# Local-attention mask: one ScalarE copy per tile instead of two TensorE products

## The reference

```python
bk2, bv2 = (look(bk), look(bv))          # keys and values of the window before and of this one
mask = (it < jb) | (it > jb + w) | (jb == -1)
sim = jnp.einsum('bhwie,bhwje->bhwij', bq, bk2) * QK_SCALE
sim = jnp.where(mask, -jnp.finfo(sim.dtype).max, sim)
attn = jax.nn.softmax(sim, -1)
```

## Time and profile before

| | |
|---|---|
| Time, median of 3 runs | 1971.37 us (1968.38 to 1974.22) |
| Profiled execution: its time, its span | 1970.89 us, 1969.1 us |
| PE, PEld busy | 1816.7 us (92%), 1289.9 us (66%) |
| DVE busy | 1503.1 us (76%) |
| ACT busy | 1322.5 us (67%) |
| POOL busy | 1397.8 us (71%) |
| Mean granted clock of TensorE | 0.991 |

### The profile page before, as it was taken

How to read it: one execution, slowest core, us unless ns; L and a number is a source line. 1 busy time by engine, 2 the same in 40 slices (tenths; PEclk the granted TensorE clock), 3 DMA queues, 4 the chain that set the end, 5 groups by cost and what they waited for, 6 DMA issues and landing times.

```text
span 1969.1 us, 70556 instructions
## 1 busy us (share of the span) xinstructions
PE 1816.7 (92%) x29444; PEld 1289.9 (66%) x29444; DVE 1503.1 (76%) x2292; ACT 1322.5 (67%) x2146; POOL 1397.8 (71%) x1492
## 2 busy tenths in 40 slices
PE   7888788789999999999999999999999999999996
PEld 5666656456667666766676666666766667667664
DVE  5866867678887887787878877778787787877873
ACT  4666767466677667666766776677767766776663
POOL 3322323888888778888778877788877888877871
PEclk9999999999999999999999999999999999999998
DMA  5000000000001000010000000000100000000000
GB/s 174 2 0 0 0 1 2 1 5 9 3 3 47 3 2 14 3 48 2 3 14 2 24 26 3 14 2 3 47 3 2 14 2 3 3 2 2 8 2 18
DMA packets 12453, 25.44 MB, mean 13 GB/s; under 512 B 1856, under 2 KB 9728, under 8 KB 10496
## 3 DMA queue, kind: packets, MB, share of 16 engines
q1 hardware_dynamic: 12160, 21.18, 3.2%
HBM read 20.13 MB, written 1.05 MB: 11 GB/s over the span
## 4 chain that ended last, share of the span: by engine, by line
PE 64%; ACT 7%; issue 7%; DVE 3%; POOL 1%; DVEq 0%; POOLq 0%; ACTq 0%
PE banks L1140 22%; PE banks L1401 15%; PE banks L1342 10%; PE banks L1425 8%; PE banks L1387 6%; PE banks L1376 2%; ACT L813 1%; ACT arena L707 1%; DVE arena L1005 1%; ACT arena L813 1%; ACT L816 1%; DVE small L1034 1%; ACT arena L718 1%; PE banks L1447 1%; ACT arena L747 0%
## 5 line engine op out<-in xcount | busy, mean ns | idle before, releaser
L1401 PE MATMUL banks<-M,xs 128*32 128x512 f32 x3072 | 367.8, 595 | 0.3 <-DVE prob L1058 0.2
L475 POOL TENSOR_TENSOR arena<-arena 128x1024 f32<-128x1024 f32 x96 | 229.8, 2394 | 152.0 <-DVE arena L1005 152.0
L747 ACT ACTIVATE arena<-banks 128x1024 f32<-128x1024 f32 x192 | 197.3, 1028 | 118.4 <-PE banks L1401 117.1
L1052 DVE TENSOR_REDUCE small<-banks 128x16 f32<-128x1024 f32 x96 | 117.5, 1224 | 203.0 <-PE banks L1387 203.0
L1000 DVE TENSOR_TENSOR arena<-banks,tabs 128x1024 f32<-128x1024 f32 x192 | 233.3, 1215 | 39.7 <-ACT arena L707 31.4
L1005 DVE TENSOR_TENSOR arena<-banks,tabs 128x1024 f32<-128x1024 f32 x192 | 232.7, 1212 | 0.0
L480 POOL TENSOR_TENSOR arena<-arena 128x1024 f32<-128x1024 f32 x96 | 229.2, 2387 | 0.0
L1425 PE MATMUL banks<-arena 128*32 128x128 f32 x6144 | 189.4, 275 | 14.6 <-DVE arena L1091 14.1
L1342 PE MATMUL banks<-cst,arena 128*128 128x128 f32 x1536 | 201.4, 274 | 0.1
L470 POOL TENSOR_TENSOR prob<-prob,small 128x1024 f32<-128x1024 f32 x96 | 184.1, 1918 | 14.0 <-DVE small L1042 14.0
L1342 PEld LDWEIGHTS banks<-cst,arena 128*128 128x128 f32 x1536 | 177.8, 141 | 23.6 <-issue 2.9
(11 more groups left out here) (130 smaller groups left out, 4135.1 us busy)
## 6 DMA issues: line engine op xcount, KB each, us to landing
arena<-in_wvo_dram SPq DMA_DIRECT2D x6, 1024.0 KB, 5.1
qkraw<-in_wqk_dram SPq DMA_DIRECT2D x6, 1024.0 KB, 4.8
W<-in_w_dram SPq DMA_DIRECT2D x6, 341.0 KB, 3.2
W<-in_w_dram SPq DMA_DIRECT2D x6, 192.0 KB, 2.4
res<-in_x_dram SPq DMA_DIRECT2D x4, 256.0 KB, 3.6
tabc<-in_tab_dram SPq DMA_DIRECT2D x1, 1024.0 KB, 9.1
out_dram<-res SPq DMA_DIRECT2D x4, 256.0 KB, 2.9
sca_s<-in_sca_dram SPq DMA_DIRECT2D x6, 128.0 KB, 4.8
```

Of the source, the lines that this page charges most:

```text
L475: pool.tensor_tensor(kc, kc, ks, ALU.add).then_inc(s["k_add"], 1)
L747: act.activation(vw[:, (2 * k + g) % RV, :], two(V_BANK), ACT.Copy).then_inc(s[f"v_cp{g}"], 1)
L1401: ins = pe.matmul(bk(V_BANK + z)[WIN * q:WIN * (q + 1), :], xs[:, b, t0:t0 + WIN], M[:, q, :, :].rearrange("p m n -> p (m n)"), start=True ...
```

## The change

`mask_scores` moves from PE to ACT. The two products of PE per tile go; ACT writes the pattern, read from the float32 constants and repeated 16 times, into banks 4 and 5 with one Copy of 1024 columns. In ACT's list it stands behind the first `gelu` and `copy_layer` and ahead of `next_folded_lower`. `scores` on PE gets a wait for it (`s_msk`). The wait of PE for ACT's copy of the upper values goes with the products; on ACT the new copy stands behind that one in the same queue. The constants `bfc`, the two activations that made them and PE's wait for them go.

```diff
-        bfc = sb("bfc", [P, P + 2 * 64], BF16)
...
-        identb = bfc[:, 0:P]
-        maskb = bfc[:, P:]
+        masks = [cst[:, C_MASK + 64 * z:C_MASK + 64 * z + 64] for z in range(2)]
...
-            def constants(z):
-
-                act.wait_ge(c_in, 16)
-                src = ident if z == 0 else cst[:, C_MASK:C_MASK + 2 * 64]
-                act.activation(identb if z == 0 else maskb, src, ACT.Copy).then_inc(s["cst_cp"], 1)
...
-                    if not more and j in (13, 15):
-                        constants((j - 13) // 2)
...
+            def mask_scores(k):
+                if is_tile(k):
+                    mask = masks[0 if tile_at(k)[1] == 0 else 1].rearrange("p (e k) -> p e k", e=1).to_broadcast([P, LH, 64])
+                    act.activation(two(4).rearrange("p (h k) -> p h k", h=LH), mask, ACT.Copy).then_inc(s["s_msk"], 1)
...
                 gelu(chunk_at(G, 10), 0)
                 copy_layer(chunk_at(G, 14))
+                mask_scores(G - 2)
                 next_folded_lower(G - 2)
...
-                        pe.wait_ge(s["cst_cp"], 2)
                         project_keys(0)
...
-            def mask_scores(k):
-
-                if is_tile(k):
-                    kind = 0 if tile_at(k)[1] == 0 else 1
-                    mask = maskb[:, 64 * kind:64 * kind + 64].rearrange("p (e k) -> p e k", e=1).to_broadcast([P, NP, 64])
-                    claim(4, 5)
-                    for o in range(2):
-                        pe.matmul(bk(4 + o).rearrange("p (k n) -> p k n", k=NP), identb, mask, start=True, stop=True)
-                    freed[4] = freed[5] = ("s_sub", k + 1)
-
             def scores(k):
                 if is_tile(k):
                     pe.wait_ge(s["kT_cp"], k + 1)
                     pe.wait_ge(s["qT_cp"], k + 1)
+                    pe.wait_ge(s["s_msk"], k + 1)
...
                     ins.then_inc(s["s_mm"], 1)
+                    freed[4] = freed[5] = ("s_sub", k + 1)
...
                 up_value(chunk_at(G, 11), 0)
-                mask_scores(G - 2)
                 transpose_probs(G - 3)
                 scores(G - 2)
```

More of the change, by code:

```diff
@@ L218, in build @@
         for n in ("k_mm q_mm kT_mm qT_mm s_mm pt_mm o_mm lnT_mm lnB_mm g_mm0 g_mm1 g_mm2 a_mm0 a_mm1 a_mm2 f_mm M_mm b1_mm v_mm0 v_mm1 xT_mm "
-                  "k_sq q_sq kT_cp qT_cp s_exp pt_cp ln_cp xn_cp xn_H y_sq y_ln y_exp gl0 gl1 gl2 xs xs_H wk_H wq_H w1_H M_H v_cp0 v_cp1 cst_cp "
+                  "k_sq q_sq kT_cp qT_cp s_exp pt_cp ln_cp xn_cp xn_H y_sq y_ln y_exp gl0 gl1 gl2 xs xs_H wk_H wq_H w1_H M_H v_cp0 v_cp1 s_msk "
                   "s_sum s_inv k_c k_s k_ss q_c q_s q_ss r_cl r_y0 r_q r_r s_max s_sub ln_x ln_bn ln_ag ln_eps "
```

## The result

The changed kernel takes 2058.61 us (median of 6 runs, 2047.35 to 2072.89), the kernel before, run beside it, 1972.8 us. The ratio is 1.042, with a 95% interval of 1.039 to 1.0451: 86 us slower. Forecast were 2070 us and a range of 2032 to 2092. The profiled execution took 2060.36 us, its span is 2058.5 us; against the profiled one of before it is 89.5 us longer. The six runs spread over 25 us, and the mean granted clock goes with them: 0.972 in the shortest, 0.965 in the longest. Its lines are shifted: the scores are L1373 now (before L1387), the mask copy is L750, the copy of the upper values L737, `copy_probs` L732, the small activations L796 and L798, the GELU L808.

A forecast was written before the change was run, and what follows sets the result against it. PE was taken to bound the loop. Late masks less the gains summed to 82.9 us, the lowered clock added net 17, so 100 us on 1970.9 gave about 2070 us, range 2032 to 2092.

The forecast's parts named there:

- The price of the copy and of the hand-over: ACT's mask copy takes 1.03 us (bounds 0.93 and 1.10), the hand-over to PE 0.06, in all 1.09 us.
- turn B: Tiles 9 to 93, every fourth: late mask costs 0.61 or 0.27 us after relief by turn A's stop; 8.8 us.
- turn A: Tiles 8 to 92, every fourth: mask behind table load, GELU and, in 20 tiles, column copies; loses 65.9 plus 4.4 us.
- turn C: Tiles 10 to 94, every fourth: gains 0.13 us 17 times (2.2 us), loses 1.09 in five tiles (5.5 us).
- turn D: Tiles 11 to 95, every fourth: mask in time, gains 7.3 us in 17; five layer ends lose 4.8 us.
- tiles 0 to 7: First tiles: one loss of some 0.9 us at each of the first three, 3 us together; bounds 0 and 6.
- The clock: PE's clock dips behind 20 of 22 long stops, 1.3 us each: 26 us, net 17, bounds 0 and 35.
- the second rival: In the loop, engines catch up while PE stands: some 40 us come back, clock holds; 2014 us, chance 0.09.
- the working's own sign: The sum is wrong if turn A's stop is shorter or the steps B to D become shorter than before.
- turn B's share: The 8.8 us loss of turn B, taken off because PE is later still after a clock dip.
- The clock did not hold: Judges the first rival: stops of 3.5 to 3.9 us come but the clock holds; +83, 2054 us, chance 0.30.
- A full price of dips in each stop: Fourth rival: a slower write, or dips in every stop at full price; up to 2100 us, chance 0.06.

The follow-up runs named there:

- the kernel with the filled stops: Changed kernel, with PE doing the transposes of the probabilities four times instead of once in steps with a first gate block; 2043.34 us, ratio 1.0336.
- the kernel with ACT's load alone: Kernel before, products kept, plus one ACT copy of 128 x 1024 per tile into a spare SBUF tile nobody reads; 2004.27 us, ratio 1.0136.
- the early place: Changed kernel, with ACT's mask copy moved directly behind its copy of the upper values; 1989.57 us, ratio 1.0073.
- the first mixed kernel: Against the kernel before: every fourth tile keeps PE's products, the others get ACT's mask directly behind the upper values' copy; 1965.71 us, ratio 0.996.

## Why the prediction was right

**The bound.** PE set the end of the loop before: without the products and without a mask 48 us came off, no less than they took. The working called 41 us the most that can be won; it left out the waits in tiles 0 to 7 that go with the products.

**The price of the copy and of the hand-over.** 1.023 us against 1.03 taken. From L750's end at 1117.86 PE's scores follow at 1118.01, 0.15 us instead of 0.06. In turn B the copy starts earlier than I had it, 0.13 us behind the start of L798 and not at its end 0.23 behind, as the activations overlap; there the two errors cancel.

**The stops.** PE's idle time right before the scores, summed over the tiles of each turn from the trace's records, against the forecast put in the same form (each loss plus the 0.43 that PE would be ready earlier):

| | forecast, us | measured, us |
|---|---|---|
| turn A, tiles 8 to 92 | 70.3 + 22 x 0.43 = 79.8 | 74.6 |
| turn B, tiles 9 to 93 | 8.8 + 20 x 0.43 = 17.4 | 15.0 |
| turn C, tiles 10 to 94 | 5.5 + 5 x 0.43 + 17 x 0.30 = 12.8 | 7.5 |
| turn D, tiles 11 to 95 | 4.8 + 5 x 0.43 = 7.0, all before the transposes | 0.9 before the scores (tile 95) |
| tiles 0 to 7 | not put in this form | 14.4 |

Turn D's term was a wait of PE's transposes for ACT's fold at the layer ends, and it stands in the list as `PE banks L1337 <- ACT M L754: 4.4, 4, 1.4`, less than taken. Of turn A's two variants one is left: the stop is 3.44 us in each of the 20 turns with column copies, where 3.55 and 3.90 were forecast, as PE's delay gives POOL time and `roots` is never late there. The relief of turn B by turn A's stop was 0.55 to 0.89 us in the working; in the kernels above the mean stop of the 20 turns B is 1.34 us without it and 0.75 with it, so 0.59.

**The clock.** The forecast was 26 us gross and 17 net, with a dip in 20 of 22 long stops; it was 19 of 22. The mean granted clock went to 0.968 (0.96 forecast), though the tenths of the clock in the page show nines as before and no eights. Gross: busy time fell by 5.5 us where the kernel without the mask has 40.7 less, so 35 us of work time came from the clock, of all dips together. Those behind turn A alone can be read from the kernel with only turn A from ACT: its steps into turn B, where nothing else changed, are 27.8 us longer. Net: filling the stops gave 16 us back. By the Trainium skill, "TensorE: Matmul & The Clock Gate", section "What's actually happening", PE falls to 1.2 GHz after an idle period; the trace agrees, with 0.62 over six microseconds behind the stop and a product at 0.63 instead of 0.39 us.

**What the sum lacked.** The result is 10 us below the forecast, and that it came no further off is in part luck: two terms that were off have opposite signs. Measured by the distance from one tile's scores to the next one's, from tile 8 on, the steps into turns A, B, C and D changed by +69.3, +37.0, -11.3 and -11.5 us in all, and tiles 0 to 7 lost 6.9 (together 90.4). Forecast were +70.3, +25.8 with the clock, +3.3, -2.5 and 3.

Turn A was right. Turn B lost 11 us more than its term. In the kernel with the filled stops its steps are 9.1 us longer in all, turn by turn 0.30 and 0.64, the working's 0.27 and 0.61; in the one with turn A alone they are 27.8 longer. Each price was right, 8.8 and 26 us; wrong was that the dips would make turn B's own loss go. The changed kernel has nearly the sum of both.

Turns C and D, which I had as a small loss, gave back 24 us more. Part of this is PE's old wait for DVE before `weigh`, 14.1 us before (L1425 on L1091) and 3.3 now:

```profile
L1412 PE MATMUL banks<-arena 128*32 128x128 f32 x6144 | 189.5, 276 | 4.3 <-DVE arena L1087 3.3
```

It is the second rival in small: work that DVE could finish while PE stood. The working held the time of the mask in these turns against the present start of the scores and let nothing come back. The kernel with turn A alone gives back 13.1 and 7.4 us in C and D, though it keeps its products there, and the kernel without any mask 17.1 and 14.4, though it has no stop: both the stop and the products that are gone elsewhere shorten these steps. How the two share the changed kernel's 23 us was not taken apart. Without the clock the sum was 83 us; the kernel with the filled stops lost 67. By the working's own sign, shorter steps in B to D, this part of it was wrong.

Tiles 0 to 7 were taken at 3 us, bounds 0 and 6, as one loss in each of the first three. In the trace of before PE waits 1.15 us for ACT's copy in each of the eight, and they lost 6.9. The upper end of the range doesn't follow from its words either: 83 + 35 and 3 for the slow write give 2092 us only if turn B's share is not taken off; with it off, 2083. The result lies well below both.

**The rivals.** The clock did not hold. The stop was given back in part, not by 40 us. From tile 8 on PE never waited for the mask in turn D but at the last tile, and in A, B and C nearly always, as the working had it. A full price of dips in each stop did not come.

**What was wrong without a cost here.** I wrote that `copy_probs` is wanted only by `weigh`. It also frees banks 2 and 3 for the transposes of the keys; the kernel with ACT's load alone lost 28 us, in the main by this. And I had thought of the queue's items between the values and the scores only as what delays the mask, not as what the mask delays: hence the missed 1945 us of the early place.

## What to carry to other kernels

An engine's idle share doesn't say whether a copy fits in; the place in its queue does. Write down, turn by turn, when the engine reaches the new item and when its result is wanted, and do the same for each item behind it: the loss (new item late) and the second loss (the next items late) are both read from the trace of before. Where one turn in four has a full queue, leave that turn on the old engine: this gave the fastest kernels that have the mask right, 0.9960 and 0.9918 of the time before. And on TensorE count a stop of a few microseconds at more than its length, since slower work follows it; 35 us of slower work came here with 87 us more idle time. Where no wait explains a loss, look for stops inside long runs of small products and at the clock behind them: a change can move them without touching their cause.

## What the runs showed of the hardware

- An ACT copy of 128 x 1024 from SBUF into PSUM took 1.023 us (median of 96), the same as one from PSUM into SBUF (1.025) and 0.026 less than one from SBUF to SBUF.
- PE's stops that the profile calls issue aren't a fixed cost. They lie mostly inside the 128 small products of the scores; before they were 34, of up to 1.2 us each, in all 24.7 us; the kernels that have the mask from ACT in most tiles, or none, had 11 to 18 of them, of up to 2.7 us. The kernel with only turn A from ACT had 10, of up to 1.1 us. With the dips they made single steps 1 to 4 us longer. The long ones come back at the same tiles in kernels with nearly the same instructions: at 57, 58, 65 and 82 in the changed kernel and in both that move its mask copy, at 61, 69, 73, 77, 81 and 89 in the three that keep turn A's products. What sets them wasn't tried.
- TensorE's clock went down to 1.2 GHz behind such stops as well as behind the waits for the mask: in the changed kernel behind 2.0 us of issue at tiles 57, 74 and 82, in the first mixed kernel six times, with a granted clock of 0.57 over the four microseconds behind the one at tile 61. Not each stop of that length has a dip behind it: the 2.34 us stops of turn A, in the kernel with the mask ahead of the column copies, had one in most turns and none in others.
